# First stage of a two-layer graph attention kernel: normalising moves from ScalarE to GpSimd, with the first mask, early query strips, a split wait and unused products

## The chip, the cores and the metric

The kernel runs on one core of a Trainium2 chip. The time is device time in microseconds (us) of one execution. The core has five engines that run their own instruction streams and meet at semaphores: TensorE (PE in the profile), VectorE (DVE), ScalarE (ACT), GpSimd (POOL) and SyncE (SP), which here only issues DMAs.

## The reference

4096 nodes with 128 features pass two layers. `adj` is a symmetric 4096x4096 matrix of 0 and 1, some 0.4% of it ones. This page is about the first layer.

```python
h = max(layernorm(x), 0)
q, k, v = h @ Wq.T + bq, h @ Wk.T + bk, h @ Wv.T + bv
scores = where(adj > 0, q @ k.T / sqrt(128), -9e15)
x = x + elu(softmax(scores) @ v)
h = max(layernorm(x), 0)               # second layer
g = h @ W
e = where(adj > 0, leaky_relu(g @ a[:128] + (g @ a[128:]).T), -9e15)
out = x + g + softmax(e) @ h
```

## The kernel before

**Stage 1, `norm_and_project`.** x comes in eight chunks of 512 nodes (four tiles of 128) by eight DMAs of SyncE. For each chunk VectorE takes the statistics (`moments_of`), ScalarE the square root (`roots`), VectorE the reciprocal and a shift (`inverse`, L170 to L176), ScalarE normalises the four tiles into `xc` (`normalise`, L114 to L119), TensorE turns them (`to_hT`), and ScalarE applies the relu on the way out (`hT_out`). Then TensorE makes the products q, k and v of the chunk into four PSUM buffers `first_pp`, at most four products ahead of the reader. ScalarE writes each product's high part (with the bias), VectorE the low part (product less high part, L380, L390, L403). Statistics run three chunks ahead, so the last of them stand in the fifth chunk. There is no scheduler: the order on each engine is the order of the code.

At the start GpSimd writes constants and issues five small DMAs: two bias columns, a bias row, two columns of `a`. ScalarE issues the four weight loads. `copy_turned` (VectorE) waits for all five small loads, scales the bias, then copies the four weights that TensorE has turned (`turn_weights`). TensorE waits for these copies before it turns the second chunk. After the last chunk, `extras` makes two small products and `copy_extras` copies them. SyncE loads the two halves of adjacency strip 0 behind x, 1 MB each.

**Stage 2, attention.** A barrier of all engines divides the stages. Stage 2 walks 32 strips of 128 queries. GpSimd turns each strip's adjacency into bytes (`mask_bytes`, L538) and these into a bfloat16 mask of 0 or -9e15 (`mask_neg`, L553). TensorE makes scores in four parts of 1024 keys (six products each, L766 to L768), two PSUM buffers in turn; VectorE adds the mask and takes the maximum (L682); ScalarE takes the exponent (L601). The weights are turned, partly by TensorE (L777, L793) and partly, for the low parts, by transposing DMAs (`turn_low`, `lowT<-low`, L502), and multiplied by v (L812, L813). `copy_q` copies each strip's queries into `q_strip` (L637). SyncE's queue is one list in program order: for the first strips it waits for the bytes of strips 0, 1 and 2 in turn, loads the next strip's adjacency after each, and only then issues the first `turn_low`. Two strips' scores are ahead of the products with v.

Stage 3, the second layer, takes the masks from a copy in DRAM and is not touched.

## Time and profile before

| | us |
|---|---|
| median of 3 runs | 785.26 (784.37 to 786.35) |
| profiled execution, its own time | 782.49 |
| span of that execution | 780.7 |

The page's first part, busy time over the span:

```profile
PE 728.9 (93%) x6229; PEld 609.6 (78%) x6229; DVE 563.2 (72%) x1199; ACT 559.9 (72%) x1095; POOL 417.6 (53%) x317
```

PE is TensorE's matmuls, PEld its weight loads, which lie beside them. The number behind each x counts instructions. Stage 1 ends near 45.5 us, stage 2 near 498 us. In the rows further down a time in the first column counts from the span's start, and the bracket at a row's end gives how long the engine sat idle before it and what released it. A row with xN merges N instructions, and its second number reaches over all of them. Matmul ends are modelled, so the distance between two starts is the better measure.

### The profile page before, as it was taken

To read this page: it belongs to the slowest core of one execution; us is meant where nothing else is said; L and a number is where in the kernel's file an instruction comes from. 1 tells how busy PE (TensorE), PEld (TensorE's weight loads), DVE (VectorE), ACT (ScalarE), POOL (GpSimd) and SP (SyncE) were. 2 spreads that over 40 slices of the span, in tenths; PEclk is the share of its full clock that TensorE was granted. 3 is DMA by queue.
4 is the path that set the end of the run, shared out by engine and by line. 5 is a ranking of instruction groups with operands and counts; after the bars stand their busy time and mean duration, and the time that the engine had idled before them with its cause. 6 is when DMAs were issued, how large, how long until landed. Compare 5 with 4: busy or idle time off the path is not lost. (4 is left out here: it accounts for less than half of the span.)

```text
span 780.7 us, 18250 instructions
## 1 busy us (share of the span) xinstructions
PE 728.9 (93%) x6229; PEld 609.6 (78%) x6229; DVE 563.2 (72%) x1199; ACT 559.9 (72%) x1095; POOL 417.6 (53%) x317
## 2 busy tenths in 40 slices
PE   4976999999999999999999998585999999999996
PEld 2555888888888888888888887463888888888885
DVE  4857687878787878878787876498585585586572
ACT  5936678687878777777868787584967977977910
POOL 1058599999999999999999973243000000000000
PEclk9988999999999999999999999797999999999999
DMA  6059989999888898989898954650234334423100
GB/s 229 1 162 280 283 212 248 274 232 280 233 280 238 271 253 254 262 247 256 255 259 245 274 112 73 123 103 1 54 69 93 81 73 91 91 64 87 37 10 13
DMA packets 189323, 130.86 MB, mean 168 GB/s; under 512 B 170336, under 2 KB 176992, under 8 KB 181088
## 3 DMA queue, kind: packets, MB, share of 16 engines
q1 hardware_dynamic: 188544, 130.05, 61.4%
q8 instruction: 24, 0.39, 0.2%
q10 hardware_dynamic: 576, 0.26, 0.1%
q14 instruction: 19, 0.16, 0.1%
q0 software_dynamic: 160, 0.00, 0.0%
HBM read 69.47 MB, written 18.87 MB: 113 GB/s over the span
## 5 line engine op out<-in xcount | busy, mean ns | idle before, releaser
L1337 PE MATMUL ps_x<-v,big 128*128 128x258 bf16 x2048 | 232.0, 275 | 2.3 <-issue 2.3
L1337 PEld LDWEIGHTS ps_x<-v,big 128*128 128x128 fp8e4 x2048 | 198.9, 98 | 32.5 <-issue 2.4
L682 DVE CUSTOM_DVE_ANT_0 scores<-ps_s,mask_neg 128x1024 f32<-128x1024 f32 x128 | 155.7, 1217 | 25.5 <-POOL mask_neg L553 17.0
L538 POOL TENSOR_SCALAR mask_bytes<-adj_sb 128x2048 uint8<-128x2048 int32 x64 | 147.5, 2321 | 44.8 <-POOLq L79 40.9
L601 ACT ACTIVATE scores<-scores,neg_max 128x1024 f32<-128x1024 f32 x128 | 146.1, 1143 | 23.3 <-DVE neg_max L688 23.3
L701 DVE TENSOR_TENSOR low<-scores 128x1024 bf16<-128x1024 f32 x96 | 136.0, 1417 | 29.2 <-ACT scores L601 27.0
L553 POOL TENSOR_SCALAR mask_neg<-mask_bytes 128x2048 bf16<-128x2048 uint8 x64 | 150.6, 2354 | 5.4 <-POOL mask_bytes L538 0.4
L812 PE MATMUL ps_acc<-v_parts,hiT 128*128 128x256 bf16 x768 | 141.6, 274 | 5.4 <-DMA lowT<-low 5.1
L615 ACT ACTIVATE hiT<-ps_t 128x512 bf16<-128x512 bf16 (+1 forms) x128 | 103.0, 805 | 56.6 <-PE ps_t L793 54.0
L878 ACT ACTIVATE big<-s_block,s_col 128x512 fp8e4<-128x512 f32 x224 | 139.3, 714 | 0.0
L813 PE MATMUL ps_acc<-v_parts,lowT 128*128 128x128 bf16 x768 | 134.7, 220 | 0.0
L766 PE MATMUL ps_s<-k_hi,q_strip 128*128 128x512 f32 x256 | 113.2, 442 | 6.2 <-DVE row_max L682 3.9
L768 PE MATMUL ps_s<-k_hi,q_strip 128*128 128x512 f32 x256 | 102.4, 400 | 0.0
L767 PE MATMUL ps_s<-k_lo,q_strip 128*128 128x512 f32 x256 | 101.2, 395 | 0.0
L812 PEld LDWEIGHTS ps_acc<-v_parts,hiT 128*128 128x128 bf16 x768 | 75.5, 98 | 13.8 <-issue 5.6
L813 PEld LDWEIGHTS ps_acc<-v_parts,lowT 128*128 128x128 bf16 x768 | 75.5, 98 | 0.7
L1272 ACT ACTIVATE sums<-ps_x,ac 128x258 f32<-128x258 f32 x64 | 26.5, 465 | 64.4 <-PE ps_x L1337 64.4
L694 DVE TENSOR_TENSOR pT_low<-ps_t,pT_high 128x512 bf16<-128x512 f32 x64 | 44.0, 688 | 31.8 <-ACT pT_high L608 31.8
L793 PE MATMUL ps_t<-ident_half,scores 128*128 128x128 bf16 x768 | 64.8, 220 | 0.0
L793 PEld LDWEIGHTS ps_t<-ident_half,scores 128*128 128x128 bf16 x768 | 44.8, 98 | 25.2 <-issue 24.8
L608 ACT ACTIVATE pT_high<-ps_t 128x512 bf16<-128x512 f32 x64 | 37.6, 589 | 35.6 <-PE ps_t L777 34.7
L766 PEld LDWEIGHTS ps_s<-k_hi,q_strip 128*128 128x128 f32 x256 | 49.4, 193 | 15.0 <-DVE row_max L682 5.0
(139 smaller groups left out, 997.3 us busy)
## 6 DMA issues: line engine op xcount, KB each, us to landing
adj_sb<-in_adj SPq DMA_DIRECT2D x64, 1024.0 KB, 5.3
mask_bytes_dram<-mask_bytes SPq DMA_DIRECT2D x32, 512.0 KB, 2.8
x_sb<-in_x SPq DMA_DIRECT2D x8, 256.0 KB, 7.7
out<-res SPq DMA_DIRECT2D x32, 64.0 KB, 1.5
lowT<-low SPq DMA_TRANSPOSE x96, 4.7
big<-mask_bytes_dram SPq DMA_TRANSPOSE x32, 4.5
raw_w<-in_L_gnn_Wq ACTq DMA_DIRECT2D x1, 64.0 KB, 3.1
raw_w<-in_L_gnn_Wk ACTq DMA_DIRECT2D x1, 64.0 KB, 3.6
```

The lines of the kernel that those rows point to most:

```text
L538: nc.gpsimd.tensor_scalar(mask_bytes[b % 2][:, half(h)], adj_sb[h][:], 1.0, 0.0, ALU.min, ALU.max).then_inc(bytes_ready, 1)
L553: nc.gpsimd.tensor_scalar(out, src, -NEG, NEG, ALU.mult, ALU.add).then_inc(mask_ready, 1)
L601: nc.scalar.activation(sc, sc, ACT.Exp, bias=neg_max[:, bn:bn + 1], accum_out=row_sum[:, bn, k:k + 1]).then_inc(exp_done, 1)
L615: nc.scalar.activation(hiT[k][:, half_of], ps_t[(2 + u) % 3][:].bitcast(BF16)[:, half_of], ACT.Copy).then_inc(hiT_ready, 1)
L682: nc.vector.tensor_tensor_reduce(out=scores[bn % 2][:, part(k)], in0=ps_s[k % 2][:], in1=mask[bn % 2][:, part(k)], scale=1.0, scalar=LOWES ...
L701: nc.vector.tensor_tensor(low[k][:], p, high_half(p), ALU.subtract).then_inc(low_done, 1)
L766: nc.tensor.matmul(o, high, k_hi[:, col], start=True, stop=False)
L793: last = nc.tensor.transpose(out[:, D * t:D * t + D], high[:, D * t:D * t + D], ident_half[:])
L812: nc.tensor.matmul(ps_a[:], high, v_parts[:, t, :, :], start=(i == 0 and n == 0), stop=False)
L813: last = nc.tensor.matmul(ps_a[:, 0, :], rest, v_parts[:, t, 0, :], start=False, stop=(i == NC - 1 and n == 3))
L878: return nc.scalar.activation(by_key_tile(lower[par], t), src.rearrange("p (s i) -> p s i", s=4), ACT.Sign, bias=s_col[:, t, 1:2], saturat ...
L1337: last = nc.tensor.matmul(ps_x[b % 2][k][:], by_key_tile(m, t)[:, b], v1[k][:, t, :].bitcast(BF16), start=(t == 0), stop=(t == T - 1))
```

## The change

- `normalise` leaves ScalarE. GpSimd does it with `tensor_scalar`, (x + shift) * rstd, where shift is now minus the mean, no longer multiplied by rstd. ScalarE's square roots of the first three chunks follow one another, and `inverse(2)` on VectorE stands ahead of `copy_turned`.
- After the eighth chunk GpSimd makes the bytes and the mask of strip 0 still in stage 1, and SyncE loads strip 1's adjacency there. The tiles of mask, bytes and query strips are allocated earlier for it.
- ScalarE copies the query strips 0 and 1 in stage 1, behind the products of chunks 1 and 2.
- The two bias loads have a semaphore of their own; `copy_turned` waits for them at its end, and ScalarE waits for the scaled bias once. The fourth weight (of the second layer) is waited for, turned and copied only at the end of the stage.
- TensorE runs 36 products of `ones` and `ident`, both 128x128 float32, into a part of PSUM that nobody reads, before it waits for the first chunk.

```diff
+WARM = 36
@@ gpsimd, norm_and_project
+            def normalise(c):
+                pool.wait_ge(inverse_ready, c + 1)
+                for t in range(4 * c, 4 * c + 4):
+                    last = nc.gpsimd.tensor_scalar(xc[:, t, :], x_sb[:, t, :], shift[:, t:t + 1], rstd[:, t:t + 1],
+                                                   ALU.add, ALU.mult)
+                last.then_inc(h_ready, 1)
+            if x_in:
+                for c in range(NC):
+                    normalise(c)
+            hook("gpsimd_end", pool)
@@ scalar
-            def normalise(c):
...
-                normalise(0)
                 roots(1)
-                normalise(1)
                 roots(2)
...
-                if x_in and c + 2 < NC:
-                    normalise(c + 2)
@@ vector, inverse
-                    nc.vector.scalar_tensor_tensor(out=shift[:, cs], in0=moments[:, cs, 0], scalar=-1.0, in1=rstd[:, cs],
-                                                   op0=ALU.mult, op1=ALU.mult).then_inc(inverse_ready, 1)
+                    nc.vector.tensor_scalar(shift[:, cs], moments[:, cs, 0], -1.0, None, ALU.mult).then_inc(inverse_ready, 1)
@@ sync, load_x
-                    sp.wait_ge(loaded, 16 * len(weights))
+                    sp.wait_ge(loaded, 16 * 3)
+                    sp.wait_ge(weight_in, 16)
                     for h in range(2):
                         sp.dma_start(adj_sb[h][:], adj_halves[0, 0, 0, h]).then_inc(adj_in[h], 16)
+                    for h in range(2):
+                        sp.wait_ge(bytes_ready, h + 1)
+                        sp.dma_start(adj_sb[h][:], adj_halves[0, 0, 1, h]).then_inc(adj_in[h], 16)
@@ gpsimd_end
+                def first_strip(pool):
+                    for h in range(2):
+                        pool.wait_ge(adj_in[h], 16)
+                        bytes_half(0, h).then_inc(bytes_ready, 1)
+                    pool.wait_ge(bytes_ready, 2)
+                    for h in range(2):
+                        mask_half(0, h).then_inc(mask_ready, 1)
@@ scalar_chunk
+                def first_strips(act, c):
+                    if c == 0:
+                        return
+                    if c <= 2:
+                        n = c - 1
+                        act.wait_ge(product_read, 1)
+                        nc.scalar.activation(q_strip[n][:, 0, :], q_hi[:, D * n:D * n + D], ACT.Copy).then_inc(q_ready, 1)
+                        nc.scalar.activation(q_strip[n][:, 1, :], q_lo[:, D * n:D * n + D], ACT.Copy).then_inc(q_ready, 1)
@@ vector_early, copy_turned
-                    dve.wait_ge(vectors_in, 16 * len(vectors))
-                    nc.vector.tensor_scalar(bias[:, 2:3], bias[:, 0:1], float(D) ** -0.5, None, ALU.mult)
...
-                    for i in range(1, 4):
+                    for i in range(1, 3):
                         nc.vector.tensor_copy(turned[i][:], pw[:, D * i:D * i + D]).then_inc(turn_read, 1)
+                    dve.wait_ge(bias_in, 16 * len(biases))
+                    nc.vector.tensor_scalar(bias[:, 2:3], bias[:, 0:1], float(D) ** -0.5, None, ALU.mult).then_inc(bias_scaled, 1)
@@ tensor, constants_in
                     pe.wait_ge(const_ready, 4)
+                    for i in range(WARM):
+                        nc.tensor.matmul(pw[:, 3 * D:4 * D], ones[:], ident[:], start=True, stop=True)
@@ tensor_end, extras
+                    pe.wait_ge(weight_in, 16)
+                    nc.tensor.transpose(pw[:, 3 * D:4 * D], raw[3][:], ident[:]).then_inc(turn_done, 1)
                     pe.wait_ge(turn_read, 4)
@@ vector_end, copy_extras
+                    dve.wait_ge(turn_done, 2)
+                    nc.vector.tensor_copy(turned[3][:], pw[:, 3 * D:4 * D]).then_inc(turn_read, 1)
```

The order on GpSimd, from the constants to stage 2 (`xc` is the normalised x; an UNCONDITIONAL_BRANCH at L79 or L80 ends the stage). Before:

```order
L316 AFFINE_SELECT ident<-ident 128x128
L318 MEMSET ones 128x128
L320 DMA bias<-in_L_gnn_bq 128x1
L320 DMA bias<-in_L_gnn_bk 128x1
L320 DMA bv_row<-in_L_gnn_bv 1x16x8
L320 DMA a_cols<-in_L_gnn_a 128x1 x2
L79 UNCONDITIONAL_BRANCH
L526 UNCONDITIONAL_BRANCH
L538 ISA
L538 TENSOR_SCALAR mask_bytes<-adj_sb 128x2048 x2
L553 TENSOR_SCALAR mask_neg<-mask_bytes 128x2048 x2
L538 TENSOR_SCALAR mask_bytes<-adj_sb 128x2048 x2
```

And now:

```order
L337 AFFINE_SELECT ident<-ident 128x128
L339 MEMSET ones 128x128
L341 DMA bias<-in_L_gnn_bq 128x1
L341 DMA bias<-in_L_gnn_bk 128x1
L343 DMA bv_row<-in_L_gnn_bv 1x16x8
L343 DMA a_cols<-in_L_gnn_a 128x1 x2
L104 TENSOR_SCALAR xc<-x_sb,shift,rstd 128x128 x32
L304 TENSOR_SCALAR mask_bytes<-adj_sb 128x2048 x2
L309 TENSOR_SCALAR mask_neg<-mask_bytes 128x2048 x2
L80 UNCONDITIONAL_BRANCH
L576 UNCONDITIONAL_BRANCH
L304 TENSOR_SCALAR mask_bytes<-adj_sb 128x2048 x2
```

The 32 tiles of x and strip 0's bytes and mask now stand ahead of the stage's end; stage 2 opens with strip 1.

The order on SyncE, from x to strip 3's adjacency. Before:

```order
L306 DMA x_sb<-in_x 128x2x256 x8
L310 DMA adj_sb<-in_adj 128x2048 x2
L79 UNCONDITIONAL_BRANCH
L482 UNCONDITIONAL_BRANCH
L487 DMA adj_sb<-in_adj 128x2048 x2
L491 DMA mask_bytes_dram<-mask_bytes 128x2048
L487 DMA adj_sb<-in_adj 128x2048 x2
L491 DMA mask_bytes_dram<-mask_bytes 128x2048
L487 DMA adj_sb<-in_adj 128x2048 x2
```

And now:

```order
L323 DMA x_sb<-in_x 128x2x256 x8
L328 DMA adj_sb<-in_adj 128x2048 x2
L331 DMA adj_sb<-in_adj 128x2048 x2
L80 UNCONDITIONAL_BRANCH
L531 UNCONDITIONAL_BRANCH
L540 DMA mask_bytes_dram<-mask_bytes 128x2048
L536 DMA adj_sb<-in_adj 128x2048 x2
L540 DMA mask_bytes_dram<-mask_bytes 128x2048
L536 DMA adj_sb<-in_adj 128x2048 x2
```

Two adjacency loads (strip 1) moved ahead of the stage's end; the store of strip 0's bytes is now the first DMA of stage 2.

The order on TensorE at the program's start (`pw` holds turned weights, `first_pt` turned x). Before:

```order
L219 MATMUL first_pt<-ident,xc 128x128 x4
L351 MATMUL pw<-ident,raw_w 128x128 x3
L351 MATMUL pw<-ident,w_next 128x128
L219 MATMUL first_pt<-ident,xc 128x128 x4
L374 MATMUL first_pp<-hT,turned_w 128x512
L384 MATMUL first_pp<-hT,turned_w 128x512
```

And now:

```order
L393 MATMUL pw<-ident,ones 128x128 x36
L220 MATMUL first_pt<-ident,xc 128x128 x4
L398 MATMUL pw<-ident,raw_w 128x128 x3
L220 MATMUL first_pt<-ident,xc 128x128 x4
L426 MATMUL first_pp<-hT,turned_w 128x512
L438 MATMUL first_pp<-hT,turned_w 128x512
```

The 36 products stand first, and the fourth weight is gone from between the two groups of transposes.

## Rows read from the trace of the kernel before

**Rows 1.** Windows by stage: us, busy us by engine (instructions), TensorE clock granted, DMA, GB/s

```profile
0.00:45.50 45.50, 31.22 (x136) 18.80 (x136) 29.66 (x113) 33.41 (x75) 3.76 (x13) 1.00 0.30 99
75.20:80.00 4.80, 4.77 (x22) 3.69 (x22) 1.52 (x1) 0.10 (x2) 4.61 (x3) 0.54 1.02 262
80.00:480.00 400.00, 400.00 (x3626) 339.57 (x3624) 318.08 (x627) 306.21 (x596) 358.52 (x261) 1.00 0.86 243
```

**Rows 2.** Timeline of the start: start us, us, engine, line, op [idle before <-releaser]

```profile
1.48 0.19 POOL L318 MEMSET ones<- 128x128 f32 x1
6.07 0.16 DVE L175 SCALAR_TENSOR_TENSOR shift<-moments,rstd 128x4 f32<-128x4 f32 x1
12.69 0.15 DVE L337 TENSOR_SCALAR bias<-bias 128x1 f32<-128x1 f32 x1 [2.98 <-DMA a_cols<-in_L_gnn_a]
13.09 0.68 DVE L343 COPY turned_w<-pw 128x128 f32<-128x128 f32 x3
13.82 1.11 PE L219 MATMUL first_pt<-ident,xc 128*128 128x128 f32 x4 [3.38 <-DVE turned_w L343]
```

**Rows 3.** Timeline of VectorE in one chunk, then a group of ScalarE by line

```profile
28.54 0.86 DVE L152 BATCH_NORM_STATS2 bn<-x_sb 128x6 f32<-128x128 f32 x4
30.16 0.75 DVE L380 SCALAR_TENSOR_TENSOR q_lo<-first_pp,bias,q_hi 128x512 f32<-128x512 f32 x1 [0.35 <-ACT q_hi L377]
31.03 0.16 DVE L175 SCALAR_TENSOR_TENSOR shift<-moments,rstd 128x4 f32<-128x4 f32 x1
32.37 0.86 DVE L152 BATCH_NORM_STATS2 bn<-x_sb 128x6 f32<-128x128 f32 x4
...
L117 ACT ACTIVATE xc<-x_sb,shift,rstd 128x128 f32<-128x128 f32 x32 | 13.2, 494 | 4.1 <-DVE shift L175 4.1
```

**Rows 4.** Timeline of TensorE in the second chunk, at full clock

```profile
19.08 0.60 PE L219 MATMUL first_pt<-ident,xc 128*128 128x128 f32 x4
19.52 1.02 PE L374 MATMUL first_pp<-hT,turned_w 128*128 128x512 f32 x2
21.23 1.05 PE L395 MATMUL first_pp<-turned_w,hT 128*128 128x128 f32 x8
22.12 0.60 PE L219 MATMUL first_pt<-ident,xc 128*128 128x128 f32 x4
```

**Rows 5.** Timeline of TensorE from the last product to the first score

```profile
42.21 1.05 PE L395 MATMUL first_pp<-turned_w,hT 128*128 128x128 f32 x8
46.06 0.79 PE L766 MATMUL ps_s<-k_hi,q_strip 128*128 128x512 f32 x1 [2.26 <-ACT q_strip L638]
```

**Rows 6.** Timeline of the ramp into attention

```profile
49.44 3.88 POOL L553 TENSOR_SCALAR mask_neg<-mask_bytes 128x2048 bf16<-128x2048 uint8 x2
51.38 1.22 DVE L682 CUSTOM_DVE_ANT_0 scores<-ps_s,mask_neg 128x1024 f32<-128x1024 f32 x1 [6.17 <-PE ps_s L768]
60.06 0.63 PE L777 MATMUL ps_t<-ident,scores 128*128 128x128 f32 x4
65.03 4.19 SPq L487 DMA_DIRECT2D adj_sb<-in_adj  x2
69.33 6.33 SPq L502 DMA_TRANSPOSE lowT<-low  x3
75.23 0.37 PE L812 MATMUL ps_acc<-v_parts,hiT 128*128 128x256 bf16 x1 [4.76 <-DMA lowT<-low]
```

**Rows 7.** Window of one us after the first scores, columns as rows 1

```profile
49.00:50.00 1.00, 1.00 (x5) 0.80 (x5) 0.00 (x0) 0.00 (x0) 0.92 (x2) 1.00 0.72 295
```

**Rows 8.** GpSimd by line: duration ns min/median/max; and two rows of the timeline

```profile
L538 POOL TENSOR_SCALAR mask_bytes<-adj_sb x64: 1883/1893/2871, 45.6 to 452.8; 128x2048 uint8<-128x2048 int32 x64
L572 POOL TENSOR_TENSOR x_sb<-x_sb,att_exp x32: 452/1377/1510, 97.3 to 494.4; 128x128 f32 x24, 128x128 f32<-128x128 f32 x8
...
97.29 1.22 DVE L701 TENSOR_TENSOR low<-scores 128x1024 bf16<-128x1024 f32 x1
97.33 1.49 POOL L572 TENSOR_TENSOR x_sb<-x_sb,att_exp 128x128 f32<-128x128 f32 x1
```

More of the change, by code:

```diff
@@ L112, in hT_out @@
                 nc.scalar.activation(hT[:, 512 * c:512 * c + 512], pt[c % 2][:], ACT.Relu, **extra).then_inc(hT_ready, 1)
-            def normalise(c):
-                act.wait_ge(inverse_ready, c + 1)
-                for t in range(4 * c, 4 * c + 4):
-                    last = nc.scalar.activation(xc[:, t, :], x_sb[:, t, :], ACT.Identity, bias=shift[:, t:t + 1],
-                                                scale=rstd[:, t:t + 1])
-                last.then_inc(h_ready, 1)
             roots(0)
@@ L292, in build, with half, bytes_half, mask_half @@
             adj_sb = [sb(first, f"adj_sb{i}", [D, N // 2], I32) for i in range(2)]
+            mask = [sb(first, f"mask_neg{i}", [D, N], BF16) for i in range(2)]
+            mask_bytes = [sb(first, f"mask_bytes{i}", [D, N], U8) for i in range(2)]
+            q_strip = [sb(first, f"q_strip{i}", [D, 2, D], F32R) for i in range(2)]
+            def half(h):
+                return slice(N // 2 * h, N // 2 * h + N // 2)
+            def bytes_half(par, h):
+                return nc.gpsimd.tensor_scalar(mask_bytes[par][:, half(h)], adj_sb[h][:], 1.0, 0.0, ALU.min, ALU.max)
+            def mask_half(par, h):
+                out = mask[par][:, half(h)].rearrange("p (g k w) -> p g k w", w=D, k=2)
+                src = mask_bytes[par][:, half(h)].rearrange("p (g w k) -> p g k w", w=D, k=2)
+                return nc.gpsimd.tensor_scalar(out, src, -NEG, NEG, ALU.mult, ALU.add)
             with ExitStack() as c1:
@@ L330, in load_weights @@
                     use_table(0, ACT.Sqrt)
-                    for dst, src in weights:
-                        act.dma_start(dst, src).then_inc(loaded, 16)
+                    for i, (dst, src) in enumerate(weights):
+                        act.dma_start(dst, src).then_inc(loaded if i < 3 else weight_in, 16)
+                def first_strips(act, c):
[6 more added lines that the diff above has]
+                        nc.scalar.activation(q_strip[n][:, 1, :], q_lo[:, D * n:D * n + D], ACT.Copy).then_inc(q_ready, 1)
                 def copy_turned(dve, steps):
-                    dve.wait_ge(vectors_in, 16 * len(vectors))
-                    nc.vector.tensor_scalar(bias[:, 2:3], bias[:, 0:1], float(D) ** -0.5, None, ALU.mult)
                     dve.wait_ge(const_ready, 3)
@@ L434, in build @@
             with ExitStack() as c2:
-                mask = [sb(c2, f"mask_neg{i}", [D, N], BF16) for i in range(2)]
                 scores = [sb(c2, f"scores{i}", [D, N], F32) for i in range(2)]
@@ L441, in build @@
                 lowT = [sb(c2, f"lowT{k}", [D, 8, D], BF16) for k in range(3)]
-                q_strip = [sb(c2, f"q_strip{i}", [D, 2, D], F32R) for i in range(2)]
                 acc_sb = sb(c2, "acc_sb", [D, 2, D], F32)
@@ L447, in build @@
                 att_exp = sb(c2, "att_exp", [D, D], F32)
-                mask_bytes = [sb(c2, f"mask_bytes{i}", [D, N], U8) for i in range(2)]
                 ps_s = [pb(c2, f"ps_s{i}", [D, PART]) for i in range(2)]
@@ L502, in turn_low @@
                         sp.dma_start(lowT[k][:], low[k][:], transpose=True).then_inc(lowT_in[k], 16)
-                    for b in range(3):
+                    store(0, 0)
+                    for b in range(2, 4):
                         for h in range(2):
-                            load(0, b + 1, h)
-                        if b < 2:
-                            store(0, b)
+                            load(0, b, h)
+                        if b == 2:
+                            store(0, 1)
                     turn_low(0, 0, 0)
@@ L537, in make_bytes @@
                                 pool.sem_inc(pool_gate, 1)
[L538 to L539 removed]
+                            bytes_half(b % 2, h).then_inc(bytes_ready, 1)
                     def make_mask(c, b):
@@ L550, in make_mask @@
                         for h in range(2):
-                            out = mask[b % 2][:, half(h)].rearrange("p (g k w) -> p g k w", w=D, k=2)
-                            src = mask_bytes[b % 2][:, half(h)].rearrange("p (g w k) -> p g k w", w=D, k=2)
-                            nc.gpsimd.tensor_scalar(out, src, -NEG, NEG, ALU.mult, ALU.add).then_inc(mask_ready, 1)
+                            mask_half(b % 2, h).then_inc(mask_ready, 1)
                     def add_halves(s):
@@ L572, in add_elu @@
                         nc.gpsimd.tensor_tensor(xs, xs, att_exp[:], ALU.add).then_inc(epi_done, 1)
-                    for b in range(3):
-                        make_bytes(0, b)
-                        if b < 2:
-                            make_mask(0, b)
+                    make_bytes(0, 1)
+                    make_mask(0, 1)
+                    make_bytes(0, 2)
                     def period(c, b):
```

40 lines of the change are left out of this document (22 added, 18 removed).

## The prediction

> **What bounds the kernel now.** I read the windows by stage first [rows 1]. The kernel has three stages: normalise and project (0 to 45.5 us), masked attention (to 498 us), and the second layer. From 80 to 480 us TensorE is busy 400.00 of 400.00 us: attention, once running, is bound by TensorE, and no edit touches that stretch. So the change can only move the moment from which TensorE runs without a wait. Before it lie 45.5 us of the first stage (TensorE busy 31.2), a ramp to 75.2 us, and 4.8 us at a granted clock of 0.54. The timeline tells why.
>
> In the first stage each of eight chunks of 512 columns takes 3.83 us (VectorE's statistics start at 28.54 and 32.37) [rows 3]. VectorE waits 0.35 us of them, for ScalarE, which is full; four of ScalarE's instructions normalise x, 13.2 us over eight chunks, 1.65 us each [rows 3]. TensorE alone needs 3.04 us a chunk (19.08 to 22.12) [rows 4]. At the start VectorE waits 2.98 us for the last small vector, and TensorE 3.38 us behind it, until 13.82 [rows 2]. In the ramp GpSimd's first mask (49.44) starts after the stage's end, VectorE waits 6.17 us until 51.38 (the row names TensorE, but the start falls on the end of the mask's first half), TensorE's first transposes of weights come at 60.06, and at 75.23 it has waited 4.76 us for a transposing DMA that stood in SyncE's queue behind two adjacency loads [rows 6].
>
> **The change part by part.**
>
> *TensorE's unused products and the early bias wait.* 36 products of 128 columns start when the ones are written, at 1.7 us [rows 2]. At full clock four such products took 0.89 us (21.23 to 22.12), 0.222 us each [rows 4]; at half clock twice that. How long is it slow? From 13.82 the first chunk took 5.26 us (to 19.08), the same instructions then 3.04 [rows 2, 4]: 2.2 us lost, so 4.4 us at half rate. After the pause of 2.26 us before 46.06 the granted clock was 1.00 again by 49 us [rows 5, 7], under 3 us. Taking 4.4: 9.9 products by 6.1 us, the other 26.1 in 5.8 us, end at 11.9. (With 2.7 us it is 11.0; never rising, 17.7.) In those rows the granted clock reads 1.00 for the whole first stage [rows 1], so there the durations must be read, not the clock. Then come four transposes of x and three of weights (0.8 us) and VectorE's three copies (0.8 us: three took 0.68 from 13.09 [rows 2], and the first waits a little for TensorE): TensorE starts the second transposes at 13.5 against 13.82. With the last vector no longer awaited, the unused products are what is late next. The gain is the clock: chunk 0 takes 3.04 instead of 5.26 us, 2.5 us in all.
>
> *Normalising on GpSimd.* No row shows a tensor_scalar of 128x128 float32 with two pointer scalars there. The 128x2048 one takes 1.893 us median, 0.92 ns a column, so 128 columns are 0.12 us plus a fixed part; the two-input 128x128 addition takes 0.452 at least and 1.510 at most [rows 8]. Ends: 0.12 and 1.51 us. I take 0.3, nearest the one-input form. Four tiles are 1.2 us a chunk, hidden under VectorE.
> The 1.49 us addition at 97.33 lies on VectorE's `low` at 97.29, which reads two SBUF tensors [rows 8]; VectorE's first stage has no long instruction like that (statistics read one tensor, the subtractions one from PSUM). The Trainium skill, Advanced Engine Details and Errata, section GPSIMD Details, says the same: GpSimd's interface conflicts with VectorE instructions that have two SBUF inputs or run in a two-port mode. By that rule 1.49 us is excluded here; by the row alone it is not, and it stays as a rival.
> GpSimd's first tensor_scalar of the kernel before starts at 45.6, as stage 2 opens, and none of the 64 takes over 2.87 us [rows 8]. The Trainium skill, GPSIMD Engine Reference, section Instruction dispatch, speaks against it: the first call of a freshly loaded library costs about 6 us. By that rule the first tiles would be ready near 13.4 instead of 7.4, the unused products cover up to 11.9, and the sum below would be 1.5 us longer; the trace does not show it.
>
> *The chunks.* ScalarE falls to 3.83 - 1.65 = 2.2 us a chunk, plus 0.4 for the query strips in two chunks: covered. VectorE becomes the bound, 3.83 - 0.35 = 3.48 us, for the chunks that carry statistics. Its first subtraction comes at 15.5: 13.5, 0.44 us of transposes, 0.86 of query products [rows 4] and 0.7 on ScalarE. Chunk 0 ends 2.2 us later (30.16 to 32.37) [rows 3], at 17.7, and four more at 31.6. TensorE, at most four products ahead, then needs two chunks of 3.04: 37.7, where the last product ended at 43.1 (42.21 + 0.89) [rows 5]. From there to the first score product it was 2.96 us (46.06); after, 0.9 longer, since the fourth weight is turned and copied behind the last subtraction, and 0.5 shorter without the strip copies: 41.0. **Gain of stage 1: 5.1 us.**
>
> *GpSimd's first mask.* The last shift comes in the fifth chunk, which starts at 28.1, 2.3 us in (28.54 to 31.19 less the wait of 0.35) [rows 3]: 30.4. Normalising ends at 31.6, bytes (2 x 1.89) and mask (3.88) at 39.3 [rows 6, 8], with 1.3 us to spare before the barrier near 40.6. SyncE's two added waits there only hold two adjacency loads, and nothing else stands in its queue; in stage 2 the loads of strip 2 then find the DMAs free.
>
> *Ramp.* With mask 0 ready VectorE follows TensorE. A score part is six products, and at full clock five began in one us (49 to 50) [rows 7]: 1.4 us with its share of waiting, as VectorE's add and maximum takes 1.22 [rows 6]. First part at half clock (the pause around 39 us may lower it) 2.5 us, second 1.5, four more at 1.4: transposes of weights at 50.7 instead of 60.06, 9.4 us earlier. From there to the product that waited, 75.23 - 4.76 - 60.06 = 10.4 us of work: 61.1. Is the transposing DMA in? GpSimd, from 40.6: bytes 1, mask 1, bytes 2 are 3.8 + 3.9 + 3.8, and 0.6 of waits: 52.7. SyncE issues two loads and then the transposing DMA at 53.4; before, issue at 69.33 was followed by the product 5.9 us later [rows 6]: 59.3, hidden by 1.8 us. So 75.23 becomes 61.1, **14.1 us**. Without that pause the 4.8 us at 0.54 clock are at full rate: 4.8 x 0.46 = **2.2 us**. Sum: 16.3 us. Everything behind is bound by TensorE and moves with it.
>
> Profiled time 782.49 (span 780.7 and 1.8 around it) - 16.3 = 766.2. The median shown is 785.26, 2.8 us above the profiled run, so on the medians' scale 785.3 - 16.3 = 769.
>
> **The rivals.**
> *A, the transposing DMA is late again (14 in 100).* For: SyncE's order is unchanged there, two loads that wait for strip 2's bytes stand ahead, and the cover is 1.8 us. Against: strip 1's 2 MB are loaded earlier. If the whole 4.76 us and the clock's 2.2 remain, the gain is 9.3: 776.
> *B, the unused products outlast x (8 in 100).* If TensorE stays at half clock they end at 17.7, 5.8 us later: gain 10.5, 775. For: the only slow start before lasted 4.4 us, so it is not sure what 36 products do. Against: it did rise each time under steady work.
> *C, GpSimd slow on single tiles, slower than before (3 in 100; 4 more for no change).* At a price p a tile, above 0.87 us GpSimd paces the chunks; the stage ends at 6.2 + 32p + 7.6 + 0.4 and the gain is 42.7 - 32p. It is nothing at p = 1.33 us and the kernel is slower from there; at the 1.51 us seen [rows 8] it loses 5.6: 791. At 1.377, the row's median: 787, within the noise. Against: the low values in the same row stand where VectorE reads one SBUF tensor.
> *D, better than forecast (9 in 100).* The clock rises after 2.7 us and does not fall between the stages: 0.9 + 1.3 us more, 767 or less, down to 764.
>
> **How the numbers follow.** Forecast 62 in 100, 769, own range 766 to 772. With A and B the range is 764 to 777; it leaves out C, no change, and the tails, some 12 in 100. About 0.3% (2.4 us) is what a measurement can tell. Forecast, A, B, D are all faster: 93; within: 4; slower: 3.
>
> **What would show it.** Unused products from 1.7 to about 12 us, the later ones 0.22 us apart. Second transposes near 13.5, chunk starts of VectorE 3.5 us apart without ScalarE as releaser. GpSimd's tiles near 0.3 us each, its masks done before VectorE's last copy. First score near 41, transposes of weights near 51, no wait of TensorE for the transposing DMA near 61, and from then on the period of before. The forecast is wrong if a tile costs over 0.87 us, if the products end past 13, if the ramp shows a wait above 2 us, or if TensorE waits between 80 and 460 us.

## The result

The changed kernel took 771.55 us (median of 4 runs, 769.68 to 773.63), the kernel before 784.82 on the same chip (4 runs, 783.59 to 786.35): ratio 0.9838, 95% interval 0.9811 to 0.9865. It is faster by 13.3 us; 16.3 were forecast, to 769.0 with a range of 764 to 777. In a second session it took 769.94 (5 runs, 768.71 to 771.91) against 784.00 (9 runs), ratio 0.9824 (0.9806 to 0.9842). The profiled runs are 769.68 (span 767.9) and 782.49 (span 780.7): 12.8 us of span to explain. The median lies just inside the forecast's own range of 766 to 772 too.

### The profile page after: what moved, and what is told of

Its sections match the earlier page's. It is cut to its first block and busy times, and to the rows that moved or that the text cites. A ratio compares the mean times of both kernels' runs of the same rounds, so it can differ in the third digit from the quotient of the medians.

```text
span 767.9 us, 18394 instructions
## 1 busy us (share of the span) xinstructions
PE 731.9 (95%) x6301; PEld 616.8 (80%) x6301; DVE 564.3 (73%) x1199; ACT 549.4 (72%) x1063; POOL 432.9 (56%) x349
## 5 line engine op out<-in xcount | busy, mean ns | idle before, releaser
L309 POOL TENSOR_SCALAR mask_neg<-mask_bytes 128x2048 bf16<-128x2048 uint8 x64 | 153.3, 2396 | 5.4 <-POOL mask_bytes L304 0.4
L661 ACT ACTIVATE hiT<-ps_t 128x512 bf16<-128x512 bf16 (+1 forms) x128 | 103.0, 805 | 53.4 <-PE ps_t L837 50.7
L810 PEld LDWEIGHTS ps_s<-k_hi,q_strip 128*128 128x128 f32 x256 | 48.9, 191 | 11.9 <-DVE row_max L726 3.3
```

The lines of the kernel that those rows point to most:

```text
L309: return nc.gpsimd.tensor_scalar(out, src, -NEG, NEG, ALU.mult, ALU.add)
L661: nc.scalar.activation(hiT[k][:, half_of], ps_t[(2 + u) % 3][:].bitcast(BF16)[:, half_of], ACT.Copy).then_inc(hiT_ready, 1)
L810: nc.tensor.matmul(o, high, k_hi[:, col], start=True, stop=False)
```

## The profile after

Below "milestones" are start times in a profile. The first copy of `ps_acc` by ScalarE, 85.48 before and 72.08 after, says when the first sum of attention is done; the last such copy, 490.97 and 477.63, says when attention ends.

First the windows by stage of the changed kernel, columns as in [rows 1].

```profile
0.00:41.70 41.70, 36.71 (x208) 27.32 (x208) 29.78 (x113) 22.96 (x46) 25.16 (x49) 1.00 0.45 158
41.70:63.90 22.20, 19.57 (x98) 14.78 (x99) 16.33 (x31) 10.08 (x16) 19.97 (x10) 0.85 0.93 265
...
80.00:460.00 380.00, 380.00 (x3424) 322.21 (x3424) 304.44 (x600) 291.09 (x571) 350.45 (x255) 1.00 0.85 246
```

From 80 to 460 us TensorE is busy all the time, as in [rows 1], and the copies of `ps_acc` come 13.32 us apart in both kernels. So nearly all of the change acted before that: the first score starts at 41.75 instead of 46.06, and 22.2 us later TensorE is at the product that had to wait for a DMA (75.23 before). (From the last such copy to the end of the profile, the third stage, it is 290.3 us instead of 289.7.)

The start of the changed kernel, timeline of several engines (start us, us, engine, line, operation, [idle before <-releaser]). L393 is the unused products, L104 GpSimd normalising, L220 the transposes of x.

```profile
1.72 10.09 PE L393 MATMUL pw<-ident,ones 128*128 128x128 f32 x72 [1.72 <-POOL ones L339]
...
6.49 1.75 POOL L104 TENSOR_SCALAR xc<-x_sb,shift,rstd 128x128 f32<-128x128 f32 x4 [1.81 <-DVE shift L177]
...
8.41 1.73 POOL L104 TENSOR_SCALAR xc<-x_sb,shift,rstd 128x128 f32<-128x128 f32 x4 [0.18 <-DVE shift L177]
...
11.65 0.60 PE L220 MATMUL first_pt<-ident,xc 128*128 128x128 f32 x4
...
13.36 0.66 PE L220 MATMUL first_pt<-ident,xc 128*128 128x128 f32 x4 [0.78 <-DVE turned_w L383]
...
16.46 0.60 PE L220 MATMUL first_pt<-ident,xc 128*128 128x128 f32 x4
```

The second transposes start at 13.36 instead of 13.82 [rows 2], and from there chunk 0 takes 3.10 us instead of 5.26. GpSimd's first four tiles take 1.75 us, 0.44 each, and no first instruction of 6 us is seen. VectorE's statistics in mid-stage:

```profile
21.39 0.86 DVE L154 BATCH_NORM_STATS2 bn<-x_sb 128x6 f32<-128x128 f32 x4
...
24.87 0.86 DVE L154 BATCH_NORM_STATS2 bn<-x_sb 128x6 f32<-128x128 f32 x4
...
28.35 0.86 DVE L154 BATCH_NORM_STATS2 bn<-x_sb 128x6 f32<-128x128 f32 x4
```

They are 3.48 us apart (3.83 in [rows 3]), with no wait for ScalarE between. The end of the stage, all engines:

```profile
36.19 3.87 POOL L309 TENSOR_SCALAR mask_neg<-mask_bytes 128x2048 bf16<-128x2048 uint8 x2
...
37.26 1.05 PE L449 MATMUL first_pp<-turned_w,hT 128*128 128x128 f32 x8
...
39.59 0.28 DVE L413 COPY turned_w<-pw 128x128 f32<-128x128 f32 x1
...
39.92 0.38 PE L408 MATMUL pw<-a_cols,turned_w 128*128 128x2 f32 x2 [1.50 <-DVE turned_w L413]
...
40.76 0.16 DVE L415 COPY wa<-pw 128x2 f32<-128x2 f32 x1 [0.89 <-PE pw L409]
...
41.75 0.47 PE L810 MATMUL ps_s<-k_hi,q_strip 128*128 128x512 f32 x1 [1.03 <-PEq L80]
```

The last products start at 37.26 (42.21 in [rows 5]), the mask is done at 40.06 (53.32 before, 49.44 + 3.88 [rows 6]), and the first score starts at 41.75. Then the ramp, where the forecast was furthest off:

```profile
52.20 0.63 PE L821 MATMUL ps_t<-ident,scores 128*128 128x128 f32 x4
...
53.02 1.89 POOL L304 TENSOR_SCALAR mask_bytes<-adj_sb 128x2048 uint8<-128x2048 int32 x1 [1.60 <-DMA adj_sb<-in_adj]
...
53.29 2.71 DVE L745 TENSOR_TENSOR low<-scores 128x1024 bf16<-128x1024 f32 x1 [1.00 <-ACT scores L647]
...
55.10 5.53 POOL L309 TENSOR_SCALAR mask_neg<-mask_bytes 128x2048 bf16<-128x2048 uint8 x2 [0.19 <-POOL mask_bytes L304]
...
55.93 1.21 DVE L726 CUSTOM_DVE_ANT_0 scores<-ps_s,mask_neg 128x1024 f32<-128x1024 f32 x1
...
56.09 6.10 SPq L551 DMA_TRANSPOSE lowT<-low  x2
...
57.20 0.79 PE L810 MATMUL ps_s<-k_hi,q_strip 128*128 128x512 f32 x1 [2.55 <-DVE row_max L726]
...
63.92 0.27 PE L856 MATMUL ps_acc<-v_parts,hiT 128*128 128x256 bf16 x1
```

The last row has no wait: [rows 6] had 4.76 us at this product. But there is a new one at 57.20, 2.55 us. TensorE needs a score buffer that VectorE's add and maximum (55.93) reads, and that stood behind `low` (53.29), which took 2.71 us instead of the 1.22 in [rows 8]. GpSimd's bytes ran from 53.02 to 54.91, and `low` ended 1.09 us behind them: it did next to nothing while they ran. Behind the wait TensorE was slow again. Windows of the same stretch (columns as in [rows 1]):

```profile
42.00:46.00 4.00, 4.00 (x13) 3.10 (x13) 1.29 (x3) 0.99 (x1) 3.92 (x3) 0.63 0.67 219
...
50.00:54.00 4.00, 4.00 (x20) 3.00 (x19) 2.79 (x7) 3.12 (x5) 2.40 (x2) 1.00 0.89 297
...
58.00:62.00 4.00, 4.00 (x34) 3.12 (x34) 4.00 (x8) 1.24 (x2) 3.92 (x2) 0.74 1.06 178
```

## The experiments

Twelve further runs follow: e11 is the changed kernel again, e5b is e5 again, and the other ten are different kernels. Where "one run" is said, the time is a single one and the argument rests on milestones of its profile. The kernel before, run once beside each group, took 781.94 us beside e1 to e4 and 786.83 beside e5, e7, e8 and e10: single times decide nothing here below some 5 us.

How far the same kernel's milestones scatter, two pairs of profiles show. The changed kernel's first score is at 41.75 and 42.79, its first copy of `ps_acc` at 72.08 and 73.86. For e5 and its repeat e5b it is 40.58 and 41.24, then 71.31 and 73.94. So differences under 3 us in the first copy of `ps_acc` count only where rows show the mechanism.

Up to the first score the scatter has one source, the moment at which the unused products end and the first transposes of x start. From there to the first score it is 30.10 us in one profile of the changed kernel (11.65 to 41.75) and 30.11 in the other (12.68 to 42.79), and 30.09 to 30.11 in e2, e3, e4 and e8, which leave this part as it is. I call it the rest of the first stage; what an edit does to it is read to some 0.02 us.

**e1: no unused products.**

```diff
-WARM = 36
+WARM = 0
```

> The changed kernel without any unused products. Theory 1 (the products are worth the clock): TensorE starts x's transposes near 8.3 instead of 11.65 us and the second transposes near 11 instead of 13.36, but at half rate: chunk 0 takes 5.2 us instead of 3.1 and ends near 16.3 (changed kernel 16.46). The first score stays within 0.5 us of 41.75: the products bring what they cost. Theory 2 (they are what gains at the start): chunk 0 ends 2 us later, near 18.5, and the first score near 43.7. Theory 3 (they only delay): chunk 0 ends near 14 us and the first score near 39.5.

One run: 772.07. Timeline of TensorE:

```profile
8.42 1.08 PE L220 MATMUL first_pt<-ident,xc 128*128 128x128 f32 x4 [8.42 <-POOL xc L104]
...
11.05 1.12 PE L220 MATMUL first_pt<-ident,xc 128*128 128x128 f32 x4 [0.91 <-DVE turned_w L383]
11.96 1.92 PE L426 MATMUL first_pp<-hT,turned_w 128*128 128x512 f32 x2
...
15.91 0.60 PE L220 MATMUL first_pt<-ident,xc 128*128 128x128 f32 x4
```

TensorE starts on x 3.2 us earlier and loses 1.76 us in a slow chunk 0 (4.86 instead of 3.10). First score 41.18, first copy of `ps_acc` 71.78: no later than with 36 products (41.75, 72.08). So theory 1 held, and in this form the edit brings nothing that the milestones show; its gain (full clock) and its price (it outlasts GpSimd's first tiles by 3 us) cancel.

**e2: 24 unused products.**

```diff
-WARM = 36
+WARM = 24
```

> 24 unused products instead of 36. In the changed kernel they end at 11.65 us while the first tiles of x are ready at 8.24; 24 should end at 9.0. Theory 1 (36 are too many, the clock rises within the first 4 us): second transposes near 11.1 (set by VectorE's third inverse at 10.2 and the copies), at full rate, chunk 0 ends near 14.2, first score near 39.6, 2.1 us earlier, span near 765.7. Theory 2 (the clock is not yet held, or VectorE's chain does not start earlier): chunk 0 at 16, first score within 0.5 us of 41.75.

One run: 771.55. They end at 9.84 at full clock; second transposes 11.54, third 14.65; first score 39.94 (1.8 earlier), transposes of weights 49.09 (3.1 earlier; granted clock 1.00 from 43 to 46, where the changed kernel had 0.63 from 42 to 46). Then TensorE and SyncE's queue:

```profile
62.46 0.37 PE L856 MATMUL ps_acc<-v_parts,hiT 128*128 128x256 bf16 x1 [3.44 <-DMA lowT<-low]
```

```profile
49.65 4.03 SPq L536 DMA_DIRECT2D adj_sb<-in_adj  x2
53.80 7.38 SPq L551 DMA_TRANSPOSE lowT<-low  x2
```

`low` was ready at 51.35, but the transposing DMA stood behind two adjacency loads until 53.80. The wait of [rows 6] is back, the clock falls to 0.58 (62 to 66 us), and the first copy of `ps_acc` comes at 72.00: 3.1 us earlier has become 0.1. Theory 1 held up to the first score and not for the span (769.6 instead of 765.7). Rival A of the forecast is real; it waits for whoever makes TensorE arrive earlier.

**e3: VectorE's first `low` behind its next add and maximum.**

```diff
                     add_mask(1, 1, 0)
+                    add_mask(1, 1, 1)
                     low_part(0, 0, 0)
-                    add_mask(1, 1, 1)
```

> The changed kernel with VectorE's add and maximum of strip 1, part 1, ahead of the low part of strip 0, part 0 (one place in the ramp). Theory 1 (TensorE's 2.55 us wait at 57.20 comes from VectorE's order: the add stood behind a low part that took 2.71 us beside GpSimd): the wait is gone, TensorE stays at full rate through 57 to 60 us, the product with v that stood at 63.92 starts 2 to 3.5 us earlier unless the transposing DMA becomes late; the first copy of the accumulator moves from 72.08 to 69 to 70.5. Theory 2 (the low part is needed as early: SyncE's transposing DMA, now issued at 56.09, moves with it): that product waits for the DMA, and the copy of the accumulator stays within 0.7 us of 72.08.

One run: 769.95. The wait at 57.2 is gone, another is there. VectorE, GpSimd and TensorE:

```profile
53.70 2.35 DVE L745 TENSOR_TENSOR low<-scores 128x1024 bf16<-128x1024 f32 x1
...
56.66 2.23 DVE L745 TENSOR_TENSOR low<-scores 128x1024 bf16<-128x1024 f32 x1
```

```profile
53.08 1.89 POOL L304 TENSOR_SCALAR mask_bytes<-adj_sb 128x2048 uint8<-128x2048 int32 x1 [1.62 <-DMA adj_sb<-in_adj]
...
55.17 5.48 POOL L309 TENSOR_SCALAR mask_neg<-mask_bytes 128x2048 bf16<-128x2048 uint8 x2 [0.19 <-POOL mask_bytes L304]
```

```profile
60.70 0.39 PE L856 MATMUL ps_acc<-v_parts,pT_high 128*128 128x256 bf16 x1 [2.62 <-DVE pT_low L738]
```

Both `low` run into GpSimd and take over 2.2 us; TensorE waits 2.62 us for what VectorE does behind them; first copy of `ps_acc` 72.55, not the 69 to 70.5 of theory 1. It is within theory 2's 0.7 us of 72.08, but not for theory 2's reason: the product with `lowT` waits for no DMA here. In these two orders VectorE decides which product waits and not how long (2.55 and 2.62 us), and the stretched `low` are the ones that meet GpSimd.

**e4: the first mask, and the load of strip 1's adjacency, at their old places in stage 2.**

```diff
-                    for h in range(2):
-                        sp.wait_ge(bytes_ready, h + 1)
-                        sp.dma_start(adj_sb[h][:], adj_halves[0, 0, 1, h]).then_inc(adj_in[h], 16)
...
+                    for h in range(2):
+                        load(0, 1, h)
...
+                    first_strip(pool)
```

> The changed kernel with strip 0's bytes and mask, and the load of strip 1's adjacency, back in stage 2; all else as changed. Theory 1 (stage 1's gain is independent, the ramp's gain is all from this part): first score stays at 41.75; transposes of weights come 14 us later as before the change (near 55.8 instead of 52.20), the product that waits for the transposing DMA near 71 (29.2 us after the first score, as before), the first accumulator copy near 81, span near 776. Theory 2 (the ramp's gain is mostly the earlier start of everything else): span near 770.

One run: 780.92. VectorE, then TensorE:

```profile
48.15 1.22 DVE L726 CUSTOM_DVE_ANT_0 scores<-ps_s,mask_neg 128x1024 f32<-128x1024 f32 x1 [6.09 <-issue]
```

```profile
42.37 0.47 PE L810 MATMUL ps_s<-k_hi,q_strip 128*128 128x512 f32 x1 [1.03 <-PEq L80]
...
49.43 0.80 PE L810 MATMUL ps_s<-k_hi,q_strip 128*128 128x512 f32 x1 [4.09 <-DVE row_max L726]
...
71.88 0.37 PE L856 MATMUL ps_acc<-v_parts,hiT 128*128 128x256 bf16 x1 [4.11 <-DMA lowT<-low]
```

The first score comes when it did (42.37; the rest of the first stage is 30.10 us), but both waits of [rows 6] are back: VectorE's for the mask, 6.09 us, with TensorE's 4.09 behind it, and TensorE's for the DMA, 4.11. The first copy of `ps_acc` is at 81.54. So the early mask and load are worth 9.5 us of the 13.4, far more than anything else in the change. (Theory 1 had the copy near 81, and the span 3 us too short.)

**e5: the fourth weight transposed and copied with the other three.**

```diff
-                    for i in range(1, 3):
+                    for i in range(1, 4):
...
-                    pe.wait_ge(weight_in, 16)
-                    nc.tensor.transpose(pw[:, 3 * D:4 * D], raw[3][:], ident[:]).then_inc(turn_done, 1)
```

> The changed kernel, but the fourth weight is turned and copied with the other three at the start, as before the change. In the changed kernel VectorE copies it behind the last subtraction (39.59), TensorE then waits 1.50 us and VectorE 0.89 us. Theory 1 (this chain holds the stage's end): the first score moves 0.8 to 1.1 us earlier, from 41.75 to near 40.8. Theory 2 (GpSimd's mask, done at 40.06, takes over as the last to reach the barrier): 0.5 us or less. In both, the start shifts by 0.2 us at most.

One run: 768.73. The 1.50 us at 39.92 are gone, first score 40.58 (1.17 earlier), first copy of `ps_acc` 71.31. The unused products ended 0.37 earlier in this profile; the rest of the first stage is 29.30 us instead of 30.10, so the edit is worth 0.8 us there. The repeat, e5b, says the same (29.29). Its time says nothing of a gain: 771.23 in the median, where the changed kernel had 769.94 beside it and theory 1 had it 1.0 to 1.2 below.

**e7: ScalarE normalises, as before; the rest as changed.** `shift` is multiplied by `rstd` for it, as before.

```diff
-                    last = nc.gpsimd.tensor_scalar(xc[:, t, :], x_sb[:, t, :], shift[:, t:t + 1], rstd[:, t:t + 1],
-                                                   ALU.add, ALU.mult)
...
+                    last = nc.scalar.activation(xc[:, t, :], x_sb[:, t, :], ACT.Identity, bias=shift[:, t:t + 1],
+                                                scale=rstd[:, t:t + 1])
```

> The changed kernel, but ScalarE normalises again (with shift = -mean x rstd), at the places it did before; GpSimd only makes strip 0's bytes and mask in stage 1. Theory 1 (the chunk's pace is what moving the tiles brought): chunks come 3.83 us apart as before instead of 3.48, plus 0.4 in the two with the query strips; TensorE's last product and the first score come 2 to 3 us later, near 44.3. GpSimd's mask is done near 26, so the barrier waits for VectorE alone, and from the first score on all is as in the changed kernel (10.5 us to the transposes of weights). Theory 2 (VectorE's pace was the bound anyway): within 0.7 us of 41.75.

One run: 775.20. First score 47.03, 5.3 us later; I expected 2 to 3. Of the 5.3, 1.0 is the later end of the unused products in this profile; the rest of the first stage is 34.4 us instead of 30.1. TensorE:

```profile
24.21 1.16 PE L451 MATMUL first_pp<-turned_w,hT 128*128 128x128 f32 x8 [1.42 <-DVE k_lo L446]
...
25.23 0.66 PE L222 MATMUL first_pt<-ident,xc 128*128 128x128 f32 x4
```

The chunks take 4.76 us (20.47 to 25.23) and 4.23 where ScalarE also has the strip copies, and then 3.83. The copies are 1.0 us of work and cost 1.3 over the pace of 3.83. First copy of `ps_acc` 77.97, 5.9 us later. That and e4's 9.5 are more than the 13.4 of the whole change: the worths of the parts overlap and can't be added.

**e8: 24 unused products, and SyncE issues the first transposing DMA ahead of the last loads.**

```diff
-                    for b in range(2, 4):
-                        for h in range(2):
-                            load(0, b, h)
-                        if b == 2:
-                            store(0, 1)
+                    for h in range(2):
+                        load(0, 2, h)
+                    store(0, 1)
+                    load(0, 3, 0)
...
+                    load(0, 3, 1)
```

> 24 unused products, and SyncE issues the first transposing DMA ahead of strip 3's second adjacency half instead of behind it. With 24 products alone TensorE waited 3.44 us for that DMA at 62.46: VectorE had the low part at 51.3, SyncE issued at 53.8. Theory 1 (SyncE's queue gives the gain of the start back): issue near 51.5, the product starts near 59.1 instead of 62.46, no wait of TensorE over 1 us, its clock stays full, the first accumulator copy near 67.5 to 69 instead of 72.0. Theory 2 (the DMA engines are full, 1.0 busy in that stretch, so that the order does not matter): the DMA lands as late, copy at 71.5 or later.

One run: 770.57. No wait for the DMA is left; here the first `low` met GpSimd's bytes and took 2.90 us, so TensorE waited 2.74 for VectorE at 55.19. First copy of `ps_acc` 69.20, 2.8 us earlier than in e2, so the milestone went theory 1's way. Of the 2.8 the last copy keeps 1.4 (477.09, e2 478.50), since one period of attention is 14.63 us long (109.25 to 123.88), and the time 1.0. Against the changed kernel, whose last copy is at 477.63, two more losses stand, and e2 has both too: the last period is 9.15 us instead of 8.20, and the half-clock stretch of the third stage is the long one (below).

**e10: the small vectors and biases awaited together again, with 24 unused products.**

```diff
+                    dve.wait_ge(bias_in, 16 * len(biases))
+                    dve.wait_ge(vectors_in, 16 * len(vectors))
...
-                    dve.wait_ge(bias_in, 16 * len(biases))
```

> 24 unused products, but VectorE waits for all five small vectors before it copies the weights, as before the change. Theory 1 (the separate wait is worth something only once the unused products end early): the last vector lands near 12.6 us, so the second transposes come near 13.9 instead of 11.54 and the first score near 42.2 instead of 39.94. Theory 2 (the vectors are in by then, since x's DMAs are spread otherwise): within 0.5 us of 39.94.

One run: 771.01. Second transposes 12.09 instead of 11.54, though the unused products ended 0.47 earlier than in e2: TensorE waits 1.79 us for VectorE's copies instead of 0.78, and the rest of the first stage is 31.09 us instead of 30.10. Waiting apart is worth 1.0 us here, between theory 1 (2.3) and theory 2 (at most 0.5): the last vector came about 1.5 us before the 12.6 that theory 1 took. In the changed kernel the unused products end so late that the joint wait would be over before the copies matter (12.09 against 13.36); I estimate its worth there at nothing.

**e9, e11, e5b and e12: four kernels, 5 rounds each, on one chip.** e11 is the changed kernel again, e5b is e5 again. e9 has 24 unused products and both e5's edit and e8's order of SyncE; e12 is e9 with 36 unused products. Beside the changed kernel e12 has

```diff
-                    for i in range(1, 3):
+                    for i in range(1, 4):
...
-                    for b in range(2, 4):
+                    for h in range(2):
+                        load(0, 2, h)
+                    store(0, 1)
+                    load(0, 3, 0)
...
+                    load(0, 3, 1)
```

and e9 also `WARM = 24`.

> 24 unused products instead of 36, the fourth weight transposed with the other three, and SyncE issues the first transposing DMA ahead of two of its loads. Theory 1 (what the start saves stays saved once the transposing DMA is issued in time): second transposes of x at 11.1 us, first score 38.6 to 39.2, the first copy of ps_acc at 68 to 69 instead of 72.1, no wait for the transposed low half there, time 766 to 768. Theory 2 (savings of the start are taken back later, by a longer stretch at half clock at the start of the third stage or by one odd period of the attention): the first copy of ps_acc at 68 to 69 too, but the time 769 to 772, no different from the changed kernel's.

> The changed kernel again, beside the others on one chip: 769.5 to 773, a ratio of 0.981 to 0.987 to the kernel before. If the length of the half-clock stretch at the start of the third stage is chance, its profile may show the longer one this time, with a time about 2 us longer.

> The fourth weight transposed with the other three, else as changed; its single run was 768.73. Theory 1 (it frees TensorE between the last product of the first stage and the first scores): 1.0 to 1.2 us shorter than the changed kernel in the medians, first score 40.6. Theory 2 (the first copy of ps_acc moves by no more than the scatter): 0 to 0.4 us shorter.

> 36 unused products as in the changed kernel, the fourth weight early, and SyncE issues the first transposing DMA ahead of two of its loads. Theory 1 (in the changed kernel the issue is hidden behind TensorE's waits for VectorE): the first copy of ps_acc at 71.0 to 71.4, as with the fourth weight early alone, time the same within 0.3 us. Theory 2 (the issue counts too, 0.42 us of wait): 70.8 to 71.0, time 0.4 us shorter. Against the run with 24 unused products it tells what the shorter start is worth by itself.

| kernel | median us (range) | ratio to before (95%) | first score | first, last copy of `ps_acc` |
|---|---|---|---|---|
| e11, changed | 769.94 (768.71 to 771.91) | 0.9824 (0.9806 to 0.9842) | 42.79 | 73.86, 479.87 |
| e5b | 771.23 (769.08 to 771.42) | 0.9833 (0.9816 to 0.9849) | 41.24 | 73.94, 479.48 |
| e12 | 770.82 (770.08 to 771.64) | 0.9836 (0.9822 to 0.9851) | 41.23 | 69.67, 477.28 |
| e9 | 767.81 (767.07 to 770.67) | 0.9809 (0.9788 to 0.9829) | 38.43 | 68.29, 475.95 |

e5b and e12 are alike until 53 us and tell the queue apart. SyncE in e5b, then in e12:

```profile
50.94 4.40 SPq L533 DMA_DIRECT2D adj_sb<-in_adj  x2
55.46 7.48 SPq L548 DMA_TRANSPOSE lowT<-low  x2
```

```profile
50.93 0.33 SPq L533 DMA_DIRECT2D adj_sb<-in_adj  x1
52.73 1.48 SPq L548 DMA_TRANSPOSE lowT<-low  x1
55.36 0.34 SPq L533 DMA_DIRECT2D adj_sb<-in_adj  x1
```

and the product that needs it:

```profile
64.17 0.37 PE L853 MATMUL ps_acc<-v_parts,hiT 128*128 128x256 bf16 x1 [3.76 <-DMA lowT<-low]
```

```profile
64.50 0.27 PE L853 MATMUL ps_acc<-v_parts,hiT 128*128 128x256 bf16 x1 [0.74 <-DMA lowT<-low]
```

(In e12 the wait is at the second such product; its first, at 60.58, had none.) In this pair the order of the queue is worth 4.3 us at the first copy of `ps_acc`, far more than the 0.4 that theory 2 gave it. The size is no constant: in e5, the same kernel as e5b, the wait for the DMA was 0.42 us and the first copy at 71.31, and against it e12 gains 1.6. There `low` met GpSimd and TensorE waited 2.28 us for VectorE instead. Of the pair's 4.3 us, 2.2 are left at the last copy, and 0.4 in the medians, which nothing can tell from none. Where does it go? e12 has periods of 14.21, 13.42, 13.54 and 13.38 in place of 13.32, 1.3 us together, and a last one of 9.00 instead of 8.20. Then the third stage: it opens at half clock in every kernel, and how long differs. One window of it in e11, then in e12, then in e9 (columns as in [rows 1]):

```profile
496.00:500.00 4.00, 4.00 (x29) 3.28 (x29) 3.48 (x7) 3.06 (x9) 1.66 (x2) 1.00 1.07 213
```

```profile
496.00:500.00 4.00, 4.00 (x24) 3.34 (x23) 2.69 (x9) 3.31 (x9) 2.22 (x2) 0.80 1.01 216
```

```profile
492.00:496.00 4.00, 4.00 (x28) 3.19 (x27) 3.63 (x7) 3.72 (x15) 2.06 (x2) 1.00 1.11 226
```

From the second to the third transposes of that stage it is 3.69 us in e11, 5.85 in e12 and 3.08 in e9. The long form also stands in the profiles of e1, e2, e4 and e8. To price it, take the time from the last copy of `ps_acc` to the end of the profile: 291.0 to 291.5 us in these four and e12, 290.1 to 290.3 in the changed kernel, e3, e5, e10 and e11, 289.2 to 289.9 in e5b, e9, e7 and the kernel before. So the long form costs about 1 us against the changed kernel's and 2 against the shortest. It does not explain why the runs of e11 lie in two groups (768.7 to 769.9 three times, 771.9 twice): the profiled run is one of the slower two, 771.88, and has the changed kernel's form. It was 1.8 us behind the first profile at the first copy already, and 2.2 at the last.

e9 keeps its lead: 2.1 us below e11 in the medians, and lower in 20 of the 25 pairs of runs. The two intervals overlap, so I call e9 the best version that ran, probably faster than the changed kernel, and not shown to be.

No run takes back the early query strips alone. The rows show only that the 2.26 us wait for `q_strip` before the first score [rows 5] is gone; what stands there now is 1.03 us at the stage's end.

## Why the prediction was right, and where it was off

The time lies in the range, and most parts came near what was forecast. The ramp did not: by the forecast's own sign, "if the ramp shows a wait above 2 us", it was wrong there.

- *Unused products* end at 11.65 (forecast 11.9) and the second transposes start at 13.36 (13.5). Right in this profile, with some luck: in the eight profiles with 36 of them they end between 11.28 and 12.68. Chunk 0 took 3.10 us (3.04). That this is "2.5 us of gain" was counted against the start of before, and hides what e1 shows: with GpSimd normalising, the first chunk would have been ready at 8.4 anyway, so the edit by itself is worth nothing that these runs show. It is rival B in a mild form that I took for the forecast.
- *GpSimd's tiles* take 0.44 us (0.3 taken), all under VectorE. The bounds of 0.12 and 1.51 held. The 1.49 us that an addition took beside `low` [rows 8] did not occur in the first stage: no tile took over 0.46. Here the rule of the Trainium skill (Advanced Engine Details and Errata, GPSIMD Details) and the trace agree, and no call of 6 us (GPSIMD Engine Reference, Instruction dispatch) is seen: the first tiles began 0.28 us after the shift began, four in 1.75 us.
- *Pace* 3.48 us, last products at 37.26 + 0.89, so 38.15 (forecast 37.7), first score 41.75 (41.0). The 0.75 us missing: 0.45 in the pace of the last chunks, and 0.3 in the fourth weight. Its path cost 1.50 + 0.89 us of waits, where I had taken 0.9 in all; e5 and e5b show its worth, 0.8 us of the first stage.
- *The first mask* was done at 40.06 (39.3), before the first score. Right, and by e4 the largest part: 9.5 us together with strip 1's load.
- *Ramp*: transposes of weights at 52.20 (50.7). 0.75 comes from the first stage. The other 0.75 is in the six score parts. They took 1.60, 2.56, 1.67, 1.69, 1.44 and 1.49 us; I had 2.5, 1.5 and four times 1.4. The half rate came behind the first part and covered eight products, 42.98 to 46.33, one and a third parts where I had one.
- *The mis-sized step* is "From there to the product that waited ... 10.4 us of work: 61.1". It was 11.72 (63.92 - 52.20). The forecast moved the stretch of before as a block, but in the new place `low` meets nearly all of one of GpSimd's bytes instructions for strip 2: `low` 2.71 instead of 1.21, TensorE waits 2.55 at 57.20, and six score products behind it run at half rate. (In the second profile of the changed kernel it is the next `low`, 58.77 to 61.53, that meets one, and TensorE waits 1.13 and then 2.19 us.) That this makes only 1.3 us more has a reason that the forecast missed too: the 10.4 us were not all work. TensorE before:

```profile
61.52 0.50 PE L766 MATMUL ps_s<-k_hi,q_strip 128*128 128x512 f32 x1 [0.83 <-DVE row_max L682]
...
64.46 0.50 PE L766 MATMUL ps_s<-k_hi,q_strip 128*128 128x512 f32 x1 [0.84 <-DVE row_max L682]
```

  With 0.26 more at 67.95 it waited 1.93 us there. The wait at 64.46 stands behind a `low` of 1.86 us (61.38 to 63.25, with GpSimd's mask running until 62.17), the same meeting in a smaller size. So the waits grew by 0.6 us, and the other 0.7 is TensorE's slower work. e3 moved the place of the wait and not its length.
- *The transposing DMA*: no wait at 63.92, as forecast, but only because TensorE was later than forecast. It was issued at 56.09 where I had 53.4: the bytes of strip 2 were done at 54.91 instead of 52.7, as their second half waited 1.60 us for its adjacency, and `low` itself only at 56.00. So the absence of the wait is luck. When TensorE came at 59.0 (e2), it waited 3.44. Rival A had 14 in 100; in variants of the changed kernel it came true in e2 and e5b (3.76), and a little in e1 (0.24), e5 (0.42) and e7 (0.94). It deserved a larger chance.
- *Clock*: the 4.8 us at 0.54 of [rows 1] are gone (clock 1.00 from 63.9 on), but 42 to 46 at 0.63 and 58 to 62 at 0.74 are left. The kernel before had two such stretches in its ramp too, which the forecast's rows didn't show: the granted clock is at half from 45.5 to 48.9 and from 52.4 to 55.8. From 75.23 to 63.92 it is 11.3 us (14.1 forecast); to the first copy of `ps_acc` it is 13.4 (16.3 forecast): the 2.1 between the two is the clock term, 2.2 as forecast.
- *All that is behind moves along*: 13.4 at the first copy, 13.3 at the last, 12.8 in the span. Right; the 0.5 lost last is in the third stage.

So: the sum was 16.3 = 5.1 + 9.0 + 2.2. Measured 4.3 + 7.0 + 2.1 = 13.4. The missing 2.9 us are 0.8 in the first stage, 2.0 in the ramp and 0.1 in the clock term.

## What to carry to other kernels

When work of a ramp moves earlier, don't move it as a block: lay the two engines that share the interface side by side at the new times, and look where a two-input instruction of VectorE now begins inside one of GpSimd's. A wait that is "hidden by 1.8 us" behind an in-order DMA queue isn't removed: each later saving of the same path will meet it, so take it out of the queue's order first. And count a gain where the steady state begins, then again at the end: between e5b and e12 4.3 us at the first sum became 2.2 at the last and 0.4 in the time. Last, before two profiles are compared, look for the one early moment that varies by itself; counted from there, the first stage repeated to 0.02 us.

## What the runs showed of the hardware

- VectorE's `low` (two SBUF inputs) that begins while a GpSimd instruction runs does next to nothing until that ends: GpSimd ends at 54.91 (changed) and 54.97 (e3), `low` at 56.00 and 56.05, 1.1 us later each time, nearly its full length of 1.21. The fourteen profiles leave no exception. Each has 96 such `low`; the 28 to 31 that begin with GpSimd idle take 1.21 to 1.23 us, and the 65 to 68 that begin inside a GpSimd instruction end 1.07 to 1.14 us behind its end, whatever their length, up to 2.93 us. In e2, `low` at 53.48 began 0.04 us before GpSimd's mask, took 1.22, and the mask's two halves took 5.82 instead of 3.87: then GpSimd waits. The Trainium skill, SBUF — State Buffer, section "SBUF: two separate sides", says that whichever starts first holds the shared ports for the whole instruction and the other blocks. These rows agree, and the price of a meeting is the rest of the other's instruction: for `low` up to 1.7 us here.
- How long TensorE is slow at the start varies from run to run of one kernel: 36 unused products took 9.9 us in one profile of the changed kernel and 10.95 in the other (from 9.55 in e5), and everything up to the first score moved with it.
- The third stage opens at half clock after a wait of TensorE of 7.50 us, in both kernels. The granted clock is at half until about 493.6 us in the changed kernel and 499.3 in e1 (windows 492 to 496 at 0.80, 496 to 500 at 0.58), and e1 was only 1.4 us behind at the last copy of `ps_acc`; what decides it stayed open, as did the cause of the single long periods of attention (14.1 to 14.7 us) in e1, e8, e9 and e12.
